# Depthwise taps moved off TensorE, four heads' scores at once, and a 64-row second pass in a four-layer block on one core

## The chip, the cores and the metric

The kernel runs on one core of a Trainium2 chip. It is measured in device microseconds for one execution (all eight images), as the median over several executions. Smaller is better. The core has five engines with a queue each: TensorE (PE in the profile, with its weight loads as PEld), VectorE (DVE), ScalarE (ACT), GpSimd (POOL) and SyncE (SP), which here issues every DMA. An engine takes its instructions strictly in the order in which the program wrote them, and semaphores join the engines.

## The reference, cut to what matters

Eight images of 384 channels and 32x32 pixels go through four layers, each `x + layer(groupnorm(x))`: attention with a depthwise term, a selective scan in four directions, a shifted blur, and a second attention. The change touches the first layer only:

```
qkvo = einsum('oc,bchw->bohw', qkvo_w, x) + qkvo_b           # C = 384
lepe = conv(v_ch, lepe_w, 5x5, 'SAME', groups=C) + lepe_b    # 25 taps for each channel
q, k, v: 12 heads of 32 channels, 1024 pixels
attn = softmax(SCALE * einsum('bnqd,bnkd->bnqk', q, k))
res = einsum('bnqk,bnkd->bnqd', attn, v) + lepe
out = einsum('oc,bchw->bohw', proj_w, res * o) + proj_b
```

Layer 1 is the selective scan: 4 directions x 384 channels x 16 states, a first-order recurrence over 1024 pixels, so 192 scans of 128 channels x 1024 pixels per image.

## The kernel before

**Stages.** All data is float32. The program is a software pipeline over images. While image i goes through its 192 scan steps (layer 1), image i+1 is taken through layer 0 ("early" events) and image i-1 through the layers 2 and 3 ("late" events). Image 0's layer 0 comes first, with nothing beside it; then seven stretches in which a scan and a layer 0 overlap; then the last image's scan with only late work beside it. Each event has a due time in scan steps (`early_events`, `late_events`, `scan_events`); `in_order` sorts them, and every engine writes its share of that one order into its queue. So nothing is dynamic: an event that waits holds up all that stands behind it on its engine.

**A scan step** i is: SP loads two rows of 1024 numbers, broadcast to 128 partitions, into `rows_b` and `rows_c` (`SLOTS` buffers each, at due times i-SLOTS+1.0 and i-SLOTS+2.3); ScalarE makes `decay` (three buffers, L1233, due i-1.25); VectorE makes `drive` = dtu x row into PSUM (L1620, due i+0.40) and runs the scan (L1630, due i+0.90); GpSimd multiplies the state by the other row (L1345), and waits for the next step's drive before it does so; TensorE transposes the product into a running sum (L984).

**Layer 0 of one image** runs three groups of four heads one after the other. Each has two stages.
- The *S stage* (14 steps): scores are made once, only for their row maxima. `S` (L855) makes two heads' 128x512 scores in PSUM banks 0 and 1, `R` (L1560, VectorE) reduces them to maxima, and the next `S` waits for that `R`. There are 32 such pairs in a group. Beside them the depthwise term is summed on TensorE in banks 2 and 3: for each of the 25 taps ScalarE makes a diagonal matrix (`dg`, L1167) and TensorE multiplies a shifted window of the padded v with it (`dw`, L902, two matmuls of 512 columns); `dh` (L1162) copies the sum into `heads`. The padded v itself comes from `tv` (eight transposes, L758) and `pv` (L1182), and `vz` (L1556) zeroes the padding once for each image.
- The *T stage* (16.2 steps): `N`, `M` and `mr` bring the maxima into a row of the moved copy of q; that row, as contraction row 33, subtracts the maximum. `T` (L875) makes transposed scores of two heads in banks 0 and 1, `E` (L1174) exponentiates them into SBUF, `V` (L886) and `Z` (L891) multiply with v and with ones, 32 columns for a head, and `O` (L1567 to L1571) divides and adds to `heads`. There are 32 `T` in a group, 16 `V` and 16 `Z`.

Once in 16 steps new step sizes are made (`x`, `d`: L957, L967, also through bank 0), and three times in an image a finished column sum is turned (`m`: L758, L1601, L1606).

Of the kernel before, what the change touches and what calls it, by code (L numbers as in the profile page):

```python
# [298 lines left out]
def build(nc, t):  # L299
    ctx = ExitStack()  # L300
    with ctx:
# [835 lines left out]
        def _(act):  # L1137
# [10 lines left out]
            def early(img, kind, a=0, j=0, scans=1, first=False):  # L1148
# [11 lines left out]
                if kind == "dh":  # L1160
                    act.wait_ge(dg_ps.h, dg_ps.at(img, TAPS * (a + 1)))
                    act.activation(heads[:, a, :], banks(2), ACT.Copy).then_inc(dh_sb.h, 1)  # L1162
                if kind == "dg":
                    m = a
                    if j >= DIAGS:
                        act.wait_ge(dg_ps.h, dg_ps.at(img, TAPS * m + j - DIAGS + 1))
                    act.activation(diag[m][j % DIAGS], ident[:, :], ACT.Copy, scale=lepe_w[:, m * TAPS + j:m * TAPS + j + 1])\  # L1167
                        .then_inc(dg_sb.h, 1)
# [629 lines left out]
```

## Time and profile before

| | us |
|---|---|
| median of 3 runs | 11385.86 (11383.32 to 11387.95) |
| the profiled execution, whole | 11378.4 |
| its span, first to last instruction | 11376.6 |
| TensorE busy | 8954.9 (79%) |
| VectorE busy | 7592.8 (67%) |
| GpSimd busy | 3956.4 (35%) |
| ScalarE busy | 3900.4 (34%) |
| granted TensorE clock, mean | 0.813 |

One stretch of the loop, from an image's first S stage to the next image's, takes 1344.8 us, and the profile shows the same length, within half a microsecond, for the last five of them.

### The profile page before, as it was taken

What the parts mean: (1) busy time and instruction counts of PE and PEld (TensorE: products, weight loads), DVE (VectorE), ACT (ScalarE), POOL (GpSimd) and SP (SyncE); (2) the same over time, 40 slices, a digit from 0 to 9 for tenths busy, and PEclk for the clock granted to TensorE, in tenths of its full rate; (3) what the DMA queues carried; (4) which work ended last, traced back from release to release, by engine and by line L of the source; (5) the groups of instructions that cost most, each with busy time, mean ns of one, the idle gap of its engine ahead of it and who ended that gap; (6) DMA issues with size and microseconds to landing.
All of it is one profiled execution on the core that took longest, in us unless ns stands there. A gap on an engine that the chain in (4) does not pass through costs nothing.

```text
span 11376.6 us, 106333 instructions
## 1 busy us (share of the span) xinstructions
PE 8954.9 (79%) x36120; PEld 4204.5 (37%) x36120; DVE 7592.8 (67%) x5637; ACT 3900.4 (34%) x4474; POOL 3956.4 (35%) x1678
## 2 busy tenths in 40 slices
PE   6985888588886888768896788858898688877556
PEld 2223333343334433344333433334333443334433
DVE  3127667866677667776668666686677766687892
ACT  1113344333333333432443334333333323343331
POOL 0004333433334333442334333343234423343560
PEclk8665888788886898778886888868898789878657
DMA  1006444744457444664447534474445744466782
GB/s 34 4 19 207 154 144 166 245 172 143 140 179 241 156 141 152 216 200 149 148 148 244 193 129 156 163 244 164 136 148 190 225 155 141 153 225 195 246 267 65
DMA packets 717974, 1876.29 MB, mean 165 GB/s; under 512 B 258897, under 2 KB 274641, under 8 KB 717265
## 3 DMA queue, kind: packets, MB, share of 16 engines
q1 hardware_dynamic: 717392, 1869.00, 49.4%
q8 instruction: 309, 5.06, 0.2%
q14 instruction: 273, 2.23, 0.1%
HBM read 1772.03 MB, written 71.04 MB: 162 GB/s over the span
## 4 chain that ended last, share of the span: by engine, by line
PE 57%; DVE 25%; issue 7%; ACT 5%; DMA 2%; DVEq 2%; SPq 1%; ACTq 1%; POOL 0%; POOLq 0%
DVE R L1630 11%; PE ps L902 9%; PE ps L875 8%; PE ps L748 8%; PE ps L855 7%; PE ps L984 7%; DVE ps L1620 6%; PE ps L886 4%; ACT R L1174 3%; PE ps L1069 3%; DVE nmx L1560 2%; PE ps L1052 2%; PE ps L891 1%; PE ps L957 1%; PE ps L981 1%
## 5 line engine op out<-in xcount | busy, mean ns | idle before, releaser
L1345 POOL TENSOR_TENSOR R<-R 128x1024 f32<-128x1024 f32 x1536 | 3659.8, 2383 | 5546.8 <-DVE ps L1620 5546.8
L1630 DVE TENSOR_TENSOR_SCAN R<-R,ps 128x1024 f32<-128x1024 f32 x1536 | 3508.1, 2284 | 440.1 <-ACT R L1233 334.1
L1233 ACT ACTIVATE R<-R,negA 128x1024 f32<-128x1024 f32 x1536 | 1749.9, 1143 | 2946.0 <-DVE R L1630 2908.6
L984 PE MATMUL ps<-ident,R 128*128 128x128 f32 x12288 | 2068.0, 327 | 588.1 <-POOL R L1345 547.5
L984 PEld LDWEIGHTS ps<-ident,R 128*128 128x128 f32 x12288 | 1746.1, 171 | 1512.1 <-POOL R L1345 753.3
L1620 DVE TENSOR_TENSOR ps<-R 128x1024 f32<-128x1024 f32 x1536 | 1993.1, 1298 | 109.3 <-DVE R L1630 4.7
L1560 DVE TENSOR_REDUCE nmx<-ps 128x2 f32<-128x1024 f32 x768 | 936.4, 1219 | 850.1 <-PE ps L855 843.9
L902 PE MATMUL ps<-R 128*128 128x512 f32 x2400 | 1258.6, 648 | 0.0
L1174 ACT ACTIVATE R<-ps 128x1024 f32<-128x1024 f32 x768 | 785.8, 1023 | 1325.6 <-PE ps L875 1325.6
L875 PE MATMUL ps<-R 33*128 33x512 f32 x3072 | 1048.0, 765 | 173.9 <-ACT R L1174 88.4
L855 PE MATMUL ps<-R 32*128 32x512 f32 x3072 | 939.4, 690 | 198.9 <-DVE nmx L1560 164.6
L748 PE MATMUL ps<-R 128*128 128x512 f32 (+1 forms) x1824 | 873.9, 637 | 202.6 <-DVE R L1498 143.5
L1567 DVE RECIPROCAL R<-ps 128x512 f32<-128x512 f32 x48 | 161.2, 3358 | 797.2 <-PE ps L891 797.2
L902 PEld LDWEIGHTS ps<-R 128*128 128x128 f32 x2400 | 434.4, 202 | 651.1 <-issue 559.3
L748 PEld LDWEIGHTS ps<-R 128*128 128x128 f32 (+1 forms) x1824 | 354.9, 199 | 661.8 <-issue 598.1
L886 PE MATMUL ps<-R 128*32 128x512 f32 x3072 | 508.6, 741 | 51.3 <-DVE R L1569 48.6
L875 PEld LDWEIGHTS ps<-R 33*128 33x128 f32 x3072 | 270.9, 215 | 703.7 <-ACT R L1174 556.0
L855 PEld LDWEIGHTS ps<-R 32*128 32x128 f32 x3072 | 243.5, 193 | 768.6 <-DVE nmx L1560 543.3
L891 PE MATMUL ps<-R,ones 128*32 128x512 f32 x3072 | 466.9, 684 | 0.0
L1337 POOL TENSOR_TENSOR R<-R 128x1024 f32<-128x1024 f32 x96 | 253.2, 2638 | 608.8 <-DVE R L1611 608.8
L1211 ACT ACTIVATE R<-ps,vecs 128x512 f32<-128x512 f32 x192 | 131.3, 684 | 802.1 <-PE ps L967 796.2
L740 PE MATMUL ps<-gn_t,group_avg 128*128 128x1 f32 x672 | 140.9, 338 | 330.4 <-DVE gn_t L1481 277.4
(154 smaller groups left out, 5749.7 us busy)
## 6 DMA issues: line engine op xcount, KB each, us to landing
R<-bc_scratch SPq DMA_DIRECT2D x3072, 512.0 KB, 4.7
R<-in_x SPq DMA_DIRECT2D x72, 512.0 KB, 6.8
out<-R SPq DMA_DIRECT2D x72, 512.0 KB, 5.2
R<-shift_scratch SPq DMA_DIRECT2D x48, 640.0 KB, 7.4
R<-R SPq DMA_DIRECT2D x192, 128.0 KB
R<-out SPq DMA_DIRECT2D x48, 512.0 KB, 8.4
R<-in_w_qkvo SPq DMA_DIRECT2D x32, 576.0 KB, 6.7
rows_scratch<-R SPq DMA_DIRECT2D x24, 512.0 KB, 7.3
```

The source lines that it names most:

```text
L748: mm = pe.matmul(dst[0:parts, hf * HALF:(hf + 1) * HALF], lhs[:, c], rhs(c, hf), start=c == 0, stop=c == NC - 1)
L855: mm = pe.matmul(ps[:, r % 2, :], q4[HD * r:HD * r + HD, g, qc * P:(qc + 1) * P], k4[HD * r:HD * r + HD, g, hf * HALF:(hf + 1) * HALF], st ...
L875: mm = pe.matmul(ps[:, bank + j, :], k2[pair][rows, kb * P:(kb + 1) * P], q2[g][pair][rows, qh * HALF:(qh + 1) * HALF], start=True, stop=True)
L886: pe.matmul(ps[HD * r:HD * r + HD, 2, :], vT[:, kb, P * g + HD * r:P * g + HD * r + HD], pT[(2 * a + r // 2) % 4][:, r % 2, :], start=kb = ...
L902: mm = pe.matmul(ps[:, 2 + hf, :], diag[m][j % DIAGS], win, start=j == 0, stop=j == TAPS - 1)
L984: mm = pe.matmul(ps[:, 4 + b // 4, (b % 4) * P:(b % 4 + 1) * P], state[i % HELD][:, b * P:(b + 1) * P], ident[:, :], start=fresh and i % G ...
L1174: act.activation(pT[a % 4].rearrange("p j q -> p (j q)"), banks(bank), ACT.Exp).then_inc(t_exp.h, 1)
L1233: act.activation(decay[i % len(decay)], dt[:, c, :], ACT.Exp, scale=negA[:, col:col + 1]).then_inc(a_sb.h, 1)
L1345: pool.tensor_tensor(state[i % HELD], state[i % HELD], rows_c[slot], ALU.mult).then_inc(hc_sb.h, 1)
L1560: v.tensor_reduce(nmx4[:, 2 * pair:2 * pair + 2, qc, hf], ps[:, 0:2, :], AX.X, ALU.max, negate=True)\
L1620: v.tensor_tensor(drive, dtu[:, c, :], rows_b[slot], ALU.mult).then_inc(b_sb.h, 1)
L1630: v.tensor_tensor_scan(h, a, b, 0.0, ALU.mult, ALU.add).then_inc(h_sb.h, 1)
```

## The change

Five things are changed in layer 0, and one in the scan.

1. `S` makes the scores of all four heads at once, in banks 0 to 3 (four matmuls of 32 rows each, 16 times a group instead of 32 times two), and `R` reduces 128x2048 at once, 16 times.
2. The taps leave TensorE. For the first 14 (`SUMMED`) ScalarE multiplies the shifted window by the tap (`dp`), the first one straight into `heads`, the others into two buffers `tapped`; GpSimd adds each of the 13 others to `heads` (`dw`, with a drain of GpSimd ahead of it). The last 11 are multiply-adds on VectorE (`dv`), spread over the T stage. `dg`, `dh` and the 25x2 matmuls of each group are gone.
3. As banks 2 and 3 hold scores now, the first `S` of a group waits until `pv` has emptied them.
4. `T` contracts over 64 rows instead of 33. The rows past 33 are zero in `k2`; `vz` zeroes one of the two `k2` buffers for each image, ahead of the padding, and SP's `q2` waits for that.
5. `pv` of a later group waits for the last `dv` of the group before.
6. `SLOTS` goes from 4 to 3: the two buffers `tapped` lie in what were the fourth row buffers.

```diff
-SB = 4 * LB
+SB = 2 * LB
-SLOTS = 4
+SLOTS = 3
-TAPS, DIAGS = 25, 8
+TAPS, SUMMED = 25, 14
...
-        for j in range(TAPS):
-            t = at + 1.0 + (S_STEPS - 1.4) * j / TAPS
-            ev += [(t - 1.0, ("dg", g, j)), (t, ("dw", g, j))]
+        for j in range(SUMMED):
+            t = at + 0.3 + (S_STEPS - 0.6) * j / SUMMED
+            ev += [(t, ("dp", g, j))] + ([(t + 1.0, ("dw", g, j))] if j else [])
...
+        ev += [(at + 0.7 + T_STEPS * j / (TAPS - SUMMED), ("dv", g, SUMMED + j)) for j in range(TAPS - SUMMED)]
...
+        tapped = [reg(at * K1, K1) for at in (15, 19)]
...
                     if a % SB:
                         pe.wait_ge(s_max.h, s_max.at(img, a))
-                    elif g:
+                    else:
+                        pe.wait_ge(lv_sb.h, lv_sb.at(img, g + 1))
+                    if a % SB == 0 and g:
                         pe.wait_ge(t_exp.h, t_exp.at(img, TB * g))
-                    for r in (2 * pair, 2 * pair + 1):
-                        mm = pe.matmul(ps[:, r % 2, :], q4[HD * r:HD * r + HD, g, qc * P:(qc + 1) * P],
+                    for r in range(GH):
+                        mm = pe.matmul(ps[:, r, :], q4[HD * r:HD * r + HD, g, qc * P:(qc + 1) * P],
                                        k4[HD * r:HD * r + HD, g, hf * HALF:(hf + 1) * HALF], start=True, stop=True)
...
-                        rows = slice(64 * j, 64 * j + HD + 1)
+                        rows = slice(64 * j, 64 * j + 64)
...
-                    for hf in range(2):
-                        win = vp[:, j // 5 + 16 * hf:j // 5 + 16 * hf + 16, j % 5:j % 5 + WW]
-                        mm = pe.matmul(ps[:, 2 + hf, :], diag[m][j % DIAGS], win, start=j == 0, stop=j == TAPS - 1)
-                    mm.then_inc(dg_ps.h, 1)
...
+                        if n > 2:
+                            act.wait_ge(dw_sb.h, dw_sb.at(img, n - 2))
+                        act.activation(tapped[n % 2].rearrange("p (h w) -> p h w", w=WW), win, ACT.Copy, scale=tap)\
+                            .then_inc(dp_sb.h, 1)
...
                     if m:
-                        act.wait_ge(dg_ps.h, dg_ps.at(img, TAPS * m))
+                        act.wait_ge(dv_sb.h, dv_sb.at(img, m))
...
+                if kind == "dw":
+                    n = (SUMMED - 1) * m + j
+                    pool.drain()
+                    pool.wait_ge(dp_sb.h, dp_sb.at(img, SUMMED * m + j + 1))
+                    pool.tensor_tensor(heads[:, m, :], heads[:, m, :], tapped[n % 2], ALU.add).then_inc(dw_sb.h, 1)
...
+                    v.wait_ge(qk_sb.h, qk_sb.at(img, 6))
+                    v.memset(k2[0], 0.0)
                     v.memset(vpad, 0.0).then_inc(vz_sb.h, 1)
...
-                    v.tensor_reduce(nmx4[:, 2 * pair:2 * pair + 2, qc, hf], ps[:, 0:2, :], AX.X, ALU.max, negate=True)\
+                    v.tensor_reduce(nmx4[:, :, qc, hf], ps[:, 0:4, :], AX.X, ALU.max, negate=True)\
...
+                if kind == "dv":
+                    m = a
+                    out = heads[:, m, :].rearrange("p (h w) -> p h w", w=WW)
+                    win = vpad.rearrange("p (h w) -> p h w", w=36)[:, j // 5:j // 5 + HH, j % 5:j % 5 + WW]
+                    v.drain()
+                    if j == SUMMED:
+                        v.wait_ge(dw_sb.h, dw_sb.at(img, (SUMMED - 1) * (m + 1)))
+                    ins = v.scalar_tensor_tensor(out, win, lepe_w[:, m * TAPS + j:m * TAPS + j + 1], out, ALU.mult, ALU.add)
```

**Place 1: VectorE in the third S stage.** Before, this is its queue (L1560 is the reduction of two heads, L1620 the drive, L1630 the scan; the names left and right of the arrow are what is written and read, and REGISTER_ALU only works out a wait's value):

```order
L1559 REGISTER_ALU
L1560 TENSOR_REDUCE nmx<-ps 128x2
L1620 TENSOR_TENSOR ps<-R 128x1024
L1559 REGISTER_ALU
L1560 TENSOR_REDUCE nmx<-ps 128x2
L1625 REGISTER_ALU
L1630 SCALAR_TENSOR_TENSOR R<-R,ps 128x1024
L1559 REGISTER_ALU
L1560 TENSOR_REDUCE nmx<-ps 128x2
L1559 REGISTER_ALU
L1560 TENSOR_REDUCE nmx<-ps 128x2
```

Of the changed kernel, the same stage (L1571 is the reduction of four heads, L1641 the drive, L1651 the scan):

```order
L1570 REGISTER_ALU
L1571 TENSOR_REDUCE nmx<-ps 128x4
L1636 REGISTER_ALU
L1641 TENSOR_TENSOR ps<-R 128x1024
L1570 REGISTER_ALU
L1571 TENSOR_REDUCE nmx<-ps 128x4
L1646 REGISTER_ALU
L1651 SCALAR_TENSOR_TENSOR R<-R,ps 128x1024
L1641 TENSOR_TENSOR ps<-R 128x1024
L1570 REGISTER_ALU
L1571 TENSOR_REDUCE nmx<-ps 128x4
```

Where two or three reductions stood around a drive and a scan, one stands now; here and there two reductions have only the drive between them.

**Place 2: GpSimd in the third S stage.** Before, only the state products (L1345):

```order
L1344 REGISTER_ALU
L1345 TENSOR_TENSOR R<-R 128x1024
L1344 REGISTER_ALU
L1345 TENSOR_TENSOR R<-R 128x1024
L1341 REGISTER_ALU
```

Of the changed kernel (L1340 is the state product, L1347 the addition of a tap):

```order
L1339 REGISTER_ALU
L1340 TENSOR_TENSOR R<-R 128x1024
L1346 REGISTER_ALU
L1347 TENSOR_TENSOR R<-R 128x1024
L1339 REGISTER_ALU
L1340 TENSOR_TENSOR R<-R 128x1024
L1346 REGISTER_ALU
L1347 TENSOR_TENSOR R<-R 128x1024
```

An addition has come between nearly every two state products.

**Place 3: VectorE in the third T stage.** Before, drives and scans alone, but for the two `O`:

```order
L1630 SCALAR_TENSOR_TENSOR R<-R,ps 128x1024
L1620 TENSOR_TENSOR ps<-R 128x1024
L1625 REGISTER_ALU
L1630 SCALAR_TENSOR_TENSOR R<-R,ps 128x1024
L1620 TENSOR_TENSOR ps<-R 128x1024
```

Of the changed kernel (L1590 is a tap's multiply-add):

```order
L1651 SCALAR_TENSOR_TENSOR R<-R,ps 128x1024
L1590 SCALAR_TENSOR_TENSOR R<-R,lepe_w 128x1024
L1641 TENSOR_TENSOR ps<-R 128x1024
L1646 REGISTER_ALU
L1651 SCALAR_TENSOR_TENSOR R<-R,ps 128x1024
L1641 TENSOR_TENSOR ps<-R 128x1024
L1590 SCALAR_TENSOR_TENSOR R<-R,lepe_w 128x1024
L1646 REGISTER_ALU
L1651 SCALAR_TENSOR_TENSOR R<-R,ps 128x1024
```

The taps stand in turn ahead of a drive, and between a drive and its scan.

## Rows read from the trace of the kernel before

**Rows 1.** The page: busy time, and the chain that ended last, by engine.

```profile
PE 8954.9 (79%) x36120; PEld 4204.5 (37%) x36120; DVE 7592.8 (67%) x5637; ACT 3900.4 (34%) x4474; POOL 3956.4 (35%) x1678
...
PE 57%; DVE 25%; issue 7%; ACT 5%; DMA 2%; DVEq 2%; SPq 1%; ACTq 1%; POOL 0%; POOLq 0%
```

**Rows 2.** Windows: start:end and length, busy us of PE, PEld, DVE, ACT, POOL, clock, DMA.

```profile
129.50:226.70 97.20, 87.73 (x229) 27.77 (x228) 39.69 (x34) 11.29 (x27) 0.00 (x0) 0.95 0.05 11
231.50:355.20 123.70, 121.46 (x384) 23.11 (x384) 4.74 (x3) 32.77 (x32) 0.00 (x0) 0.51 0.00 0
...
595.80:698.20 102.40, 92.88 (x229) 29.00 (x228) 39.45 (x33) 11.30 (x27) 0.00 (x0) 0.88 0.01 2
703.30:828.40 125.10, 122.79 (x384) 23.24 (x384) 4.74 (x3) 32.77 (x32) 0.00 (x0) 0.50 0.00 0
5398.80:5511.20 112.40, 99.31 (x545) 35.81 (x546) 68.94 (x40) 59.54 (x60) 44.57 (x19) 0.91 0.54 178
5644.60:5759.10 114.50, 105.99 (x540) 35.29 (x540) 66.46 (x38) 60.76 (x63) 44.50 (x19) 0.88 0.53 176
5886.80:6001.10 114.30, 107.24 (x533) 36.72 (x533) 66.43 (x38) 58.75 (x59) 44.59 (x19) 0.84 0.48 166
5258.50:5393.40 134.90, 117.78 (x369) 46.45 (x368) 91.93 (x66) 34.53 (x54) 37.30 (x16) 0.89 0.36 123
5517.30:5639.30 122.00, 108.83 (x357) 44.08 (x356) 89.76 (x66) 33.62 (x52) 35.19 (x15) 0.91 0.34 117
5764.40:5881.50 117.10, 103.09 (x337) 41.02 (x336) 89.31 (x64) 32.84 (x51) 35.19 (x15) 0.92 0.35 124
```

**Rows 3.** Groups by line: engine, operation, count, busy us, mean ns, idle before.

```profile
L902 PE MATMUL ps<-R 128*128 128x512 f32 x2400 | 1258.6, 648 | 0.0
...
L1560 DVE TENSOR_REDUCE nmx<-ps 128x2 f32<-128x1024 f32 x768 | 936.4, 1219 | 850.1 <-PE ps L855 843.9 <-issue 1.0
...
L1182 ACT ACTIVATE R<-ps,vecs 128x1024 f32<-128x1024 f32 x24 | 27.1, 1128 | 151.8 <-PE ps L758 97.5 <-DVE R L1556 54.4
```

**Rows 4.** Steps of the scan alone: two drives in order of time.

```profile
6095.65 1.23 DVE L1620 TENSOR_TENSOR ps<-R 128x1024 f32<-128x1024 f32 x1
...
6099.38 1.23 DVE L1620 TENSOR_TENSOR ps<-R 128x1024 f32<-128x1024 f32 x1
```

**Rows 5.** An S stage in order of time: start us, length, what, idle before and releaser.

```profile
5262.57 2.08 PE L855 MATMUL ps<-R 32*128 32x512 f32 x4 [2.94 <-DVE nmx L1560]
...
5274.90 1.28 DVE L1601 SCALAR_TENSOR_TENSOR R<-R,derived,ps 128x1024 f32<-128x1024 f32 x1 [4.43 <-PE ps L758]
...
5334.79 2.36 POOL L1345 TENSOR_TENSOR R<-R 128x1024 f32<-128x1024 f32 x1
...
5336.26 1.98 DVE L1620 TENSOR_TENSOR ps<-R 128x1024 f32<-128x1024 f32 x1
...
5338.15 1.21 DVE L1560 TENSOR_REDUCE nmx<-ps 128x2 f32<-128x1024 f32 x1
...
5339.29 2.27 DVE L1630 TENSOR_TENSOR_SCAN R<-R,ps 128x1024 f32<-128x1024 f32 x1
```

**Rows 6.** Single lines: shortest, median and longest in ns.

```profile
L1620 DVE TENSOR_TENSOR ps<-R x1536: 1216/1234/3881, 937.4 to 11095.7; 128x1024 f32<-128x1024 f32 x192
...
L1586 DVE SCALAR_TENSOR_TENSOR R<-R,derived x24: 1283/1285/3108, 846.2 to 10076.4; 128x1024 f32<-128x1024 f32 x24
```

**Rows 7.** Image 0, first T stage, in order of time.

```profile
273.60 2.08 PE L875 MATMUL ps<-R 33*128 33x512 f32 x4
...
277.48 2.08 PE L875 MATMUL ps<-R 33*128 33x512 f32 x4
```

**Rows 8.** A loop T stage at full clock, in order of time.

```profile
5704.68 1.13 PE L875 MATMUL ps<-R 33*128 33x512 f32 x4
...
5707.99 1.06 PE L886 MATMUL ps<-R 128*32 128x512 f32 x8
```

**Rows 9.** The loads of the drive's rows (SP, L599): issue to landing.

```profile
DMA to landing us min/median/max: 3.2/4.7/13.1
```

More of the change, by code:

```diff
@@ L380, in build @@
         vpad = side(14336, 36 * 36)
-        diag = [[side(9216 + K1 * g + P * i, P) for i in range(DIAGS)] for g in range(GROUPS0)]
         rinv = [side(HALF * i, HALF) for i in range(2 * GROUPS0)]
@@ L472, in build @@
         pv_ps = sem("products_done", GROUPS0 * TB // 2)
-        dg_sb = sem("tap_diagonal_ready", TAPS * GROUPS0)
-        dg_ps = sem("tap_summed", TAPS * GROUPS0)
-        dh_sb = sem("depthwise_term_ready", GROUPS0)
+        dp_sb = sem("tap_product_ready", SUMMED * GROUPS0)
+        dw_sb = sem("tap_summed", (SUMMED - 1) * GROUPS0)
+        dv_sb = sem("depthwise_term_ready", GROUPS0)
         o_sb = sem("heads_divided", 2 * GROUPS0)
@@ L667, in early @@
                     if g == 0:
-                        sp.wait_ge(s_ps.h, s_ps.at(img, 1))
+                        sp.wait_ge(vz_sb.h, vz_sb.at(img, 1))
                         for pair in range(2):
@@ L845, in early @@
                 if kind == "S":
-                    g, qc, hf, pair = a // SB, a % SB // 4, a % 4 // 2, a % 2
+                    g, qc, hf = a // SB, a % SB // 2, a % 2
                     if a == 0:
@@ L879, in early @@
                     g, qh, kb = a // (2 * LB), a // LB % 2, a % LB
-                    if kb == 0 and qh == 0:
-                        pe.wait_ge(dh_sb.h, dh_sb.at(img, g + 1))
                     if kb == 0 and qh == 1:
@@ L1159, in early @@
                             .then_inc(qk_sb.h, 1)
[L1160 to L1168, printed above, removed]
+                if kind == "dp":
+                    m, n = a, (SUMMED - 1) * a + j
+                    win = vpad.rearrange("p (h w) -> p h w", w=36)[:, j // 5:j // 5 + HH, j % 5:j % 5 + WW]
+                    tap = lepe_w[:, m * TAPS + j:m * TAPS + j + 1]
+                    if j == 0:
+                        act.wait_ge(lv_sb.h, lv_sb.at(img, m + 1))
+                        act.activation(heads[:, m, :].rearrange("p (h w) -> p h w", w=WW), win, ACT.Copy, scale=tap)\
+                            .then_inc(dp_sb.h, 1)
+                    else:
+                        if n > 2:
+                            act.wait_ge(dw_sb.h, dw_sb.at(img, n - 2))
+                        act.activation(tapped[n % 2].rearrange("p (h w) -> p h w", w=WW), win, ACT.Copy, scale=tap)\
+                            .then_inc(dp_sb.h, 1)
                 if kind == "E":
@@ L1352, in late @@
                     norm(img, u)
-            norm(0, "attn0")
-            norm(0, "scan")
+            for ev in in_order(early_events()):
+                if ev[0] == "ne":
+                    norm(0, ev[1])
+                elif ev[0] == "dw":
+                    early(0, *ev)
             for ev in in_order(first_scan_events()):
@@ L1363, in _ @@
                     norm(1, ev[1])
+                elif ev[0] == "dw":
+                    early(1, *ev)
             with pool.Fori(1, B - 1) as img:
@@ L1369, in _ @@
                         norm(img + 1, ev[1])
+                    elif ev[0] == "dw":
+                        early(img + 1, *ev)
                     elif is_late(ev):
@@ L1565, in early @@
                     v.wait_ge(pv_ps.h, pv_ps.at(img, LB * (a + 1)))
-                    v.wait_ge(dh_sb.h, dh_sb.at(img, g + 1))
+                    v.wait_ge(dw_sb.h, dw_sb.at(img, (SUMMED - 1) * (g + 1)))
                     v.reciprocal(rinv[a], ps[:, 3, :])
@@ L1711, in _ @@
             v.memset(negm[:, :], 0.0)
+            v.memset(k2[1], 0.0)
             v.memset(ones[:, :], 1.0)
```

14 lines of the change are left out of this document (6 added, 8 removed).

## The prediction

> **What bounds the kernel now.** I read the page first, then windows cut at the stages, then single lines in order of time. TensorE is busy for 79% of the span and holds 57% of the chain that ended last, VectorE 25% [rows 1]. That is a mean over stages, so I read each stage by itself. In the three S stages of a loop image TensorE is busy 118, 109 and 103 us of 135, 122 and 117, VectorE about 90 to 92 in each [rows 2]. There the two alternate: a reduction, then the next scores, and between scores the tap matmuls, 50 in a group (2400 rows are 24 groups x 50 x 2, as a float32 matmul shows as two rows, 0.65 us each) [rows 3]. VectorE idles before L1560 for 850 us in total, nearly all of it until L855 is done [rows 3]. So the S stages are bound by TensorE. In the T stages TensorE is busy 99 to 107 of 112 to 114 us and VectorE 66 to 69 [rows 2]: TensorE again, with some 45 us of slack on VectorE. Outside both (some 640 of an image's 1344.8 us) nothing of the change but the row buffers counts.
>
> **The granted clock.** The S and T stages of the loop run at 0.84 to 0.92 on average, so 16 to 32% of a stage is at 1.2 GHz. Image 0's T stages are the odd ones: TensorE is busy for 121.5 of 123.7 us and yet the clock is 0.51, while the S stage ahead of it has 0.95 [rows 2]. `T` takes 2.08 us there and one `T` with its `V` or `Z` 3.87 us [rows 7], where at full clock they take 1.13 and 1.06 [rows 8]. What stands in those stages is `T` on 33 rows of a tile and `V`, `Z` on 32 columns, and no full-size matmul.
>
> **The change, part by part.** I sum against the profiled execution, 11378.4 us, which lies 7.5 under the median.
>
> *S stage in the loop (21 of them).* Off TensorE go 50 tap matmuls and half of the score passes. What is left for it in a step is one transposed product and 1.14 score passes, so VectorE sets the pace. A step of scan alone takes 3.73 us (two drives) [rows 4]; a reduction of 128x1024 takes 1.14 until the next instruction starts [rows 5], so one of 128x2048 about 2.25 (not over twice 1.14, not under 1.9). 14 x 3.73 + 16 x 2.25 = 88 us. To that come:
> - the third stage: 1.4 for a dt sum and the minimum. As TensorE is little busy, I expect 1.2 GHz, where scores take 2.08 [rows 5]. Where only the drive stands between two reductions (twice in a stage, place 1) VectorE waits about 1 us; two step-size matmuls put 1.5 each in that path. GpSimd's additions: below, 6. Sum 88 + 1.4 + 2 + 3 + 6 = 100.5.
> - the second: a column merge besides, 2.5 busy and 7 waiting (4.43 before L1601 now [rows 5], more at the lower clock): 110.
> - the first: two row projections more. It is 12.9 us longer than the second now [rows 2], a part of it being the zeroing; I keep 8: 118.
>
> Together 328.5 against 374.0 [rows 2], so 45 less for each image, 7 images: **-315**. Bounds: VectorE's own busy time and no waits give -70 for an image, every wait doubled -20.
>
> *GpSimd against VectorE.* A drive that starts while GpSimd runs is held: 1.98 us instead of 1.23, its end 1.1 after GpSimd's; the longest is 3.88; L1586, like `dv` a multiply-add with two SBUF inputs, goes from 1.28 to 3.11. The scan and the reductions beside it keep their length [rows 5, 6]. In a step of the new S stage GpSimd starts the state product when the drive ends (2.36 us), then the addition (2.36, the same form), so it is free 4.8 us after the drive. VectorE comes to the next drive after scan and reduction, 2.28 + 2.25 = 4.5 us. So I charge 0.25 for a step and 2.4 once, where two additions stand between two state products: 6 us. The drain of GpSimd shows in no row; I take it as free, and at the most as 1 us. ScalarE's 14 products of about 1.13 us (L1182, the nearest) [rows 3] replace 25 short ones and find it busy 33 to 35 us of a stage [rows 2]: hidden.
>
> *Start of a group.* The first scores now wait for `pv`, 1.13 us, and for the zeroing of `k2` in front of it. 5 us in the first group, 1.5 in the others: 8 x 8 = **+64**. Bounds 2 and 12 for an image.
>
> *T stage.* 11 `dv` a group. Six stand ahead of a drive (GpSimd's product just ends, 1.4 us each), five between a drive and its scan, where GpSimd starts first: 1.28 + 2.3 = 3.6 each. 26 us onto 66 leaves VectorE at 92 of 114. TensorE still sets the pace; as decays and `E` share ScalarE's queue a part will leak: +3 a stage, x 21 = +63 (bounds 0 and 10). On 64 rows `T` does the same passes in the same time. If the rows also bring the clock up, what is at 1.2 GHz now (2 x 0.09 x 112, 2 x 0.12 x 114, 2 x 0.16 x 114 = 84 us in an image, of which 39 are the cold starts after `N`) loses half of 45: -22 an image. With VectorE as full as that I take half, -11 x 7 = -78. Sum **-15**.
>
> *Image 0.* S stage: 16 x (2.25 + 2.08 + 0.1) = 71 against a mean of 100 [rows 2, 5]: **-87**. T stage at full clock: 32 x 2.25 = 72, plus the wait for `O`, 76 against 124: **-144**.
>
> *Three row buffers.* A row lands 4.7 us after its issue in the median and 13.1 at the longest [rows 9]. Three steps of scan alone are 11.2 us, less one drive 10, so the median is covered and the tail, in the late-layer loads, isn't: 4 us an image, **+32** (bounds 0 and 80).
>
> **Sum.** -315 + 64 - 15 - 87 - 144 + 32 = -465: 11378.4 - 465 = 10,913, and 10,920 on the median's scale.
>
> **On the clock,** the Trainium skill ("TensorE: Matmul & The Clock Gate", Part 1) says that the gate follows how busy TensorE has been. By that rule image 0's T stages, 98% busy, should have had the full clock; the trace shows 0.51. So the rule as it stands doesn't decide this case. If busy time were all, 64 rows would change nothing, which is the second rival below.
>
> **The rivals.**
> - *The clock doesn't follow the rows* (0.27). For it: nothing in the trace has 64-row tiles, and `V` and `Z`, half of the time, stay as they are. Against it: image 0's S stages, with full-size tap matmuls, run at 0.88 to 0.95 and its T stages at 0.51 [rows 2]. It takes away 144 and 78: 11,140.
> - *VectorE bounds the T stage* (0.10). 92 of 114 us is a mean; if the `dv` that stand between drive and scan pass half of their 18 us on, a T stage gains nothing from the clock and grows by 10: +210 instead of -15, 11,145.
> - *Four row tiles don't run side by side* (0.04). For it: the trace has only pairs. Against it: `V` puts four column tiles through in 1.06 us [rows 8]. If four took twice as long, a score pass would be 4.2 us at 1.2 GHz, against 3.5 that a drive and a scan cover: 1 us more for each of 16 passes in 21 stages, 2.1 in image 0's three, +436: 11,350, about as before.
> - *GpSimd becomes the bound of the S stage, and the kernel is slower* (0.05). The chain is drive, state product, addition, drive: 1.23 + 2.36 + 2.36 = 5.95 us with nothing between [rows 5]. Fourteen are 83 us, with merges and projections 95. An S stage is 124.7 now, and the other terms (-150) give 7 us more to each, so the kernel is slower from (131.8 - 95) / 13 = 2.8 us of drain and hand-over for an addition on; at 3.5 us it takes 11,560. Against it: where one engine hands over to another in the S stage, scores to a reduction, it costs about 0.1 us. For it: no row has a drain of GpSimd.
> - The rest (0.02) is no visible change.
>
> **How the numbers follow.** My case has 0.52. Its own range comes from the bounds of the S stage (-175, +175), taken half, and of the row buffers: 10,740 to 11,060. Two rivals lie at 11,140, so the range that leaves out 2 in 10 is 10,680 (every S wait hidden, and the T stages' clock gain whole) to 11,180. A measurement of this kernel tells about 0.2% (23 us) from no change. Faster: 0.52 + 0.27 + 0.10 + 0.03 for the tiles = 0.92; same 0.02; slower 0.05 for GpSimd and 0.01 for the tiles = 0.06.
>
> **What would show it.** Right: VectorE's idle time before the reductions falls from 850 us to under 200; S stages of 118, 110 and 100 us with a granted clock of 0.5 to 0.6; reductions of about 2.3 us; GpSimd busy about 740 us more (312 additions x 2.36) and drives held by a few tenths; image 0's T stages of 76 us at a clock near 0.95. Wrong: T stages of image 0 still at 0.51; drives of 3 us in the S stages; scans that wait for row loads; T stages over 120 us.

## The result, and the profile after

| | before | after |
|---|---|---|
| median, us | 11384.59 (4 runs, 11382.62 to 11387.95) | 10545.74 (4 runs, 10530.69 to 10569.52) |
| profiled execution, whole | 11378.4 | 10569.5 |
| ratio of the medians | | 0.9265, 95% interval 0.9246 to 0.9283 |

The changed kernel is 839 us (7.4%) faster; the forecast was 10,920 with a range of 10,680 to 11,180. The sign was right, and the gain was not quite twice the forecast. The profiled execution is the longest of the four, 24 us over the median, so a term read from its trace is good to some 20 us.

The page of the changed kernel: busy time, and the chain that ended last by engine (to compare with [rows 1]).

```profile
PE 7395.8 (70%) x33720; PEld 3735.7 (35%) x33720; DVE 8085.9 (77%) x5526; ACT 4057.7 (38%) x4186; POOL 4790.4 (45%) x1990
...
PE 41%; DVE 31%; issue 14%; ACT 7%; DMA 4%; DVEq 2%; SPq 1%; ACTq 1%; POOL 0%; POOLq 0%
```

TensorE lost 1559 us of work, VectorE took 493 more, GpSimd 834 more. VectorE is now the busiest engine. The windows of image 0's first S and T stage, then of one loop image's three S stages and its three T stages (columns as in [rows 2]):

```profile
132.80:205.10 72.30, 33.44 (x128) 8.27 (x128) 36.91 (x17) 15.99 (x14) 30.49 (x13) 0.50 0.07 15
210.00:282.50 72.50, 68.92 (x384) 15.89 (x384) 15.08 (x13) 32.63 (x32) 0.00 (x0) 0.95 0.00 1
4799.80:4905.60 105.80, 62.20 (x268) 27.95 (x268) 90.35 (x48) 39.96 (x41) 67.66 (x28) 0.71 0.44 146
5028.80:5128.80 100.00, 59.64 (x256) 30.20 (x256) 90.20 (x49) 39.27 (x39) 71.04 (x28) 0.64 0.43 145
5245.90:5342.10 96.20, 55.33 (x236) 26.75 (x236) 87.85 (x48) 38.60 (x38) 72.05 (x28) 0.61 0.48 157
4911.00:5021.80 110.80, 97.71 (x545) 34.46 (x546) 90.50 (x51) 59.51 (x60) 43.45 (x19) 0.93 0.48 171
5134.10:5238.60 104.50, 95.66 (x540) 32.61 (x540) 89.32 (x49) 60.72 (x63) 42.25 (x18) 0.98 0.52 178
5347.70:5455.00 107.30, 96.55 (x533) 34.25 (x533) 87.92 (x49) 58.49 (x59) 43.80 (x19) 0.94 0.53 177
```

In the S stages TensorE fell from 103 to 118 us busy to 55 to 62, and VectorE fills 88 to 90 of 96 to 106: the bound changed hands. In the T stages TensorE still sets the pace, at a granted clock of 0.93 to 0.98 instead of 0.84 to 0.91, and VectorE rose from 66 to 69 us to 88 to 91. Image 0's T stage went from 123.7 us at 0.51 to 72.5 at 0.95.

Two groups of the page (columns as in [rows 3]):

```profile
L1571 DVE TENSOR_REDUCE nmx<-ps 128x4 f32<-128x2048 f32 x384 | 877.0, 2284 | 298.8 <-PE ps L858 295.2
...
L1347 POOL TENSOR_TENSOR R<-R 128x1024 f32<-128x1024 f32 x312 | 822.9, 2637 | 401.5 <-ACT R L1162 339.8
```

VectorE's idle time before the reductions fell from 850 us to 299, not under 200. GpSimd's 312 additions took 823 us.

**The span by stages.** An S stage runs here from a group's first scores to the end of its minimum (L1595), a T stage from its first `T` to its last `Z`; image 0 ends with the first scan; the loop is seven images. All are from profiled executions, in us. The last image's scan, 1193 to 1197 in all, makes up the span.

| kernel | median | span | image 0 | loop S stage, mean of 21 | loop T stage, mean of 21 | rest of the loop |
|---|---|---|---|---|---|---|
| before | 11384.6 | 11376.6 | 941.4 | 124.7 | 113.2 | 4246 |
| b_rows64 | 11097.0 | 11104.8 | 792.9 | 125.2 | 106.9 | 4246 |
| b_slots3 | 11400.3 | 11399.1 | 954.0 | 124.9 | 114.4 | 4227 |
| after | 10545.7 | 10567.7 | 709.7 | 100.2 | 107.0 | 4310 |
| a_rows33 | 10833.2 | 10825.4 | 867.3 | 100.0 | 112.6 | 4300 |
| a_pairs | 11310.7 | 11300.8 | 820.9 | 131.3 | 106.5 | 4292 |
| a_smalladds | 10493.9 | 10500.4 | 708.6 | 98.0 | 106.3 | 4306 |
| a_dvahead | 10545.8 | 10537.3 | 710.1 | 100.2 | 106.2 | 4299 |
| a_dvbetween | 10663.6 | 10665.7 | 708.3 | 100.0 | 108.5 | 4384 |
| a_steps12 | 10539.4 | 10537.1 | 709.7 | 96.1 | 107.4 | 4359 |
| a_dv12 | 10475.0 | 10469.8 | 710.4 | 96.0 | 107.6 | 4290 |
| a_dv10 | 10504.0 | 10501.4 | 708.1 | 89.8 | 112.3 | 4357 |
| a_tv0 | 10524.2 | 10518.5 | 704.9 | 100.8 | 106.8 | 4262 |
| a_dvtv | 10481.7 | 10491.4 | 703.9 | 97.9 | 108.1 | 4268 |

From before to after, over unrounded stages: S stages of the loop -516, T stages -128, image 0 -232, rest of the loop +63, last image +3, together -809.

### The profile page after: what moved, and what is told of

The parts are those of the page before. It is cut to its first block, busy times and chain, and to the rows that moved or that the text cites. A ratio compares the mean times of both kernels' runs of the same rounds, so it can differ in the third digit from the quotient of the medians.

```text
span 10567.7 us, 101292 instructions
## 1 busy us (share of the span) xinstructions
PE 7395.8 (70%) x33720; PEld 3735.7 (35%) x33720; DVE 8085.9 (77%) x5526; ACT 4057.7 (38%) x4186; POOL 4790.4 (45%) x1990
## 3 DMA queue, kind: packets, MB, share of 16 engines
q14 instruction: 289, 2.36, 0.1%
## 4 chain that ended last, share of the span: by engine, by line
PE 41%; DVE 31%; issue 14%; ACT 7%; DMA 4%; DVEq 2%; SPq 1%; ACTq 1%; POOL 0%; POOLq 0%
DVE R L1651 14%; PE ps L749 8%; DVE ps L1641 7%; PE ps L878 7%; PE ps L975 5%; ACT R L1169 4%; DVE nmx L1571 3%; PE ps L1060 3%; PE ps L887 3%; PE ps L858 3%; PE ps L948 2%; PE ps L1043 2%; PE ps L958 1%; PE ps L843 1%; PE ps L1032 1%
## 5 line engine op out<-in xcount | busy, mean ns | idle before, releaser
L1340 POOL TENSOR_TENSOR R<-R 128x1024 f32<-128x1024 f32 x1536 | 3676.4, 2394 | 4304.6 <-DVE ps L1641 4194.3
L1651 DVE TENSOR_TENSOR_SCAN R<-R,ps 128x1024 f32<-128x1024 f32 x1536 | 3507.8, 2284 | 178.9 <-ACT R L1228 65.8
L975 PE MATMUL ps<-ident,R 128*128 128x128 f32 x12288 | 2153.8, 336 | 584.0 <-POOL R L1340 542.2
L1641 DVE TENSOR_TENSOR ps<-R 128x1024 f32<-128x1024 f32 x1536 | 2025.4, 1319 | 163.0 <-DMA R<-bc_scratch 56.7
L858 PE MATMUL ps<-R 32*128 32x512 f32 x3072 | 687.3, 979 | 754.6 <-DVE nmx L1571 662.3
L1571 DVE TENSOR_REDUCE nmx<-ps 128x4 f32<-128x2048 f32 x384 | 877.0, 2284 | 298.8 <-PE ps L858 295.2
L878 PE MATMUL ps<-R 64*128 64x512 f32 x3072 | 917.8, 676 | 204.9 <-ACT R L1169 107.2
L1347 POOL TENSOR_TENSOR R<-R 128x1024 f32<-128x1024 f32 x312 | 822.9, 2637 | 401.5 <-ACT R L1162 339.8
L1590 DVE SCALAR_TENSOR_TENSOR R<-R,lepe_w 128x1024 f32<-128x1024 f32 x264 | 512.7, 1942 | 28.1 <-issue 6.2
L858 PEld LDWEIGHTS ps<-R 32*128 32x128 f32 x3072 | 172.7, 266 | 994.6 <-DVE nmx L1571 844.8
L1162 ACT ACTIVATE R<-R,lepe_w 128x1024 f32<-128x1024 f32 x312 | 360.7, 1159 | 352.9 <-POOL R L1347 352.8
L878 PEld LDWEIGHTS ps<-R 64*128 64x128 f32 x3072 | 244.2, 194 | 641.9 <-ACT R L1169 418.0
L887 PE MATMUL ps<-R 128*32 128x512 f32 x3072 | 432.2, 636 | 55.2 <-DVE R L1580 51.4
L1332 POOL TENSOR_TENSOR R<-R 128x1024 f32<-128x1024 f32 x96 | 253.0, 2636 | 441.6 <-DVE R L1632 441.6
L759 PE MATMUL ps<-ident,R 128*128 128x128 f32 x1280 | 215.4, 325 | 231.1 <-DVE R L1670 71.5
```

Of the source, the lines that this page charges most:

```text
L858: mm = pe.matmul(ps[:, r, :], q4[HD * r:HD * r + HD, g, qc * P:(qc + 1) * P], k4[HD * r:HD * r + HD, g, hf * HALF:(hf + 1) * HALF], start= ...
L878: mm = pe.matmul(ps[:, bank + j, :], k2[pair][rows, kb * P:(kb + 1) * P], q2[g][pair][rows, qh * HALF:(qh + 1) * HALF], start=True, stop=True)
L887: pe.matmul(ps[HD * r:HD * r + HD, 2, :], vT[:, kb, P * g + HD * r:P * g + HD * r + HD], pT[(2 * a + r // 2) % 4][:, r % 2, :], start=kb = ...
L975: mm = pe.matmul(ps[:, 4 + b // 4, (b % 4) * P:(b % 4 + 1) * P], state[i % HELD][:, b * P:(b + 1) * P], ident[:, :], start=fresh and i % G ...
L1340: pool.tensor_tensor(state[i % HELD], state[i % HELD], rows_c[slot], ALU.mult).then_inc(hc_sb.h, 1)
L1347: pool.tensor_tensor(heads[:, m, :], heads[:, m, :], tapped[n % 2], ALU.add).then_inc(dw_sb.h, 1)
```

## The experiments

Names that begin with b_ are the kernel before with a part of the change, those with a_ the changed kernel with an edit. Ratios are to the kernel before on the same chip.

**b_rows64: the 64-row second pass alone** (with the zeroing of `k2` and SP's wait for it).

```diff
-                        rows = slice(64 * j, 64 * j + HD + 1)
+                        rows = slice(64 * j, 64 * j + 64)
```

> The kernel before with the 64-row second pass alone (and the zeroing that it needs). Theory: the gain in the T stages comes from the clock, and the rows alone bring it: image 0's T stages fall from 124 us at 0.51 to about 73 near 1.0 (-153), the loop's T stages from a mean of 114 to 105 or below, since no taps wait on VectorE there (-9 x 21 = -190): about 11,040. Rival: the T stages became shorter since TensorE, ScalarE and PSUM no longer carry taps ahead of them; then 64 rows alone change nothing: 11,384.

Measured 11097.0 (11093.3 to 11106.6), ratio 0.9747 [0.973, 0.9763]. Its windows of image 0's first T stage and of the loop's third:

```profile
236.30:307.90 71.60, 68.22 (x384) 15.87 (x384) 4.74 (x3) 32.74 (x32) 0.00 (x0) 0.96 0.00 1
...
5689.60:5794.00 104.40, 93.67 (x533) 32.20 (x533) 66.41 (x38) 58.48 (x59) 44.53 (x19) 0.97 0.54 182
```

The same 384 matmul rows as before, in 71.6 us at 0.96 instead of 123.7 at 0.51. The first rival (the clock doesn't follow the rows) fell; the theory stands, if some 60 us short of its number. Image 0 gave 148 us, the 21 T stages 132, and the S stages took 9 back. The zeroing of `k2` takes 0.91 us once for each image, in the first S stage. It doesn't account for the 9 us: the first S stages became 3.3 us shorter, the second and third 1.6 and 2.9 longer. Why is open.

**a_rows33: the changed kernel on 33 rows**, the same edit backwards.

> The changed kernel with the second pass back on 33 rows. Theory of the clock: image 0's T stages return to 124 us at 0.51 (+155) and the loop's to 113 or more (+6 x 21 = +126): 10,545 + 281 = 10,826. Rival, that the rows do nothing: 10,545.

Measured 10833.2 (10827.2 to 10836.5), ratio 0.9517 [0.9501, 0.9533]. Image 0's first T stage and the loop's third:

```profile
210.70:335.50 124.80, 122.56 (x384) 23.32 (x384) 15.10 (x12) 32.76 (x32) 0.00 (x0) 0.50 0.00 1
...
5549.90:5664.40 114.50, 107.72 (x533) 37.35 (x533) 87.93 (x49) 58.71 (x59) 43.94 (x19) 0.83 0.49 166
```

So the rows are worth 288 us in either kernel: this part adds to the others and doesn't depend on them.

**b_slots3: three row buffers alone** (`SLOTS = 3`).

> The kernel before with three row buffers instead of four, nothing else. Theory now: the drives and products have enough lead with three, within 5 us of before (11,384). Rival, as predicted: 4 us for each image, 11,416.

Measured 11400.3 (11389.2 to 11411.9), ratio 1.0012 [1.0003, 1.0022], so +14 (0.3 to 2.2 in a thousand). It lies between the two. Drives that never waited for a row before now do so 23 times, for 54 us in all; most of that was slack. Nor are the 14 us shown to come from rows: in the traces, 22 us apart, 12.6 us of the difference lie in image 0, which ends with the first scan, so before any drive.

**a_pairs: scores of two heads at a time, all else as in the changed kernel.**

```diff
-SB = 2 * LB
+SB = 4 * LB
...
-                    for r in range(GH):
-                        mm = pe.matmul(ps[:, r, :], q4[HD * r:HD * r + HD, g, qc * P:(qc + 1) * P],
+                    for r in (2 * pair, 2 * pair + 1):
+                        mm = pe.matmul(ps[:, r % 2, :], q4[HD * r:HD * r + HD, g, qc * P:(qc + 1) * P],
```

> The changed kernel with the scores of two heads at a time again (32 passes and 32 reductions a group), taps as changed. Theory: the width of the reduction matters as much as the taps, as each pass exposes a round trip to TensorE at the lower clock: image 0's S stage is 32 x (1.23 + 2.1 + 0.1) = 110 instead of 72 (+113), the loop's S stages 118 instead of 100 (+380): 11,040. Rival: with the taps gone TensorE has room, reductions of either width fill VectorE alike, and it costs under 3 us a stage: below 10,610 plus what image 0 loses.

Measured 11310.7 (11293.8 to 11334.7), ratio 0.994 [0.9923, 0.9957]: 765 us above the changed kernel, and 214 above b_rows64. The 214 us are what moving the taps does by itself (with the later start and three row buffers): it makes the kernel slower. The third S stage, a pair's scores and VectorE's reductions in it:

```profile
5678.10:5803.50 125.40, 94.44 (x236) 37.48 (x236) 88.79 (x63) 38.34 (x38) 66.28 (x28) 0.50 0.36 123
```

```profile
5692.35 2.08 PE L858 MATMUL ps<-R 32*128 32x512 f32 x4
```

```profile
L1571 DVE TENSOR_REDUCE nmx<-ps 128x2 f32<-128x1024 f32 x32 | 39.2, 1225 | 36.6 <-PE ps L858 36.6
```

With the tap matmuls, full-size, this stage ran at 0.92 before and at 0.90 in b_rows64; without them the granted clock is 0.50, where a pair's scores take 2.08 us, and the reductions of the 32 rounds wait 36.6 us for scores, against 27.8 before. Sixteen rounds of four heads wait 7.1. That the lower clock makes the difference between 27.8 and 36.6 is read from these rows; no run changes the clock alone. I expected 11,040. That had the lower clock in it and image 0 right (110 us a stage for 109), but the 118 us for the loop's S stages were not worked out, and they took 131. Those 131 us, above the 125 of the kernel before, are the clearest evidence that moving the taps pays only together with four heads at a time.

**a_smalladds: GpSimd's additions on 8 of 1024 columns.**

```diff
-pool.tensor_tensor(heads[:, m, :], heads[:, m, :], tapped[n % 2], ALU.add)
+pool.tensor_tensor(heads[:, m, 0:8], heads[:, m, 0:8], tapped[n % 2][:, 0:8], ALU.add)
```

> The changed kernel, but each of GpSimd's tap additions adds 8 of 1024 columns, so the depthwise term is left incomplete; waits, order and ScalarE's products stay. Theory: the additions cost VectorE only the holding of drives, 2.5 us an S stage in the loop (drives took 20.8 us where 15 x 1.22 are 18.3), 21 stages: 10,545 - 53 = 10,490; image 0 unchanged. Rival, as predicted, GpSimd's share is 6 us a stage or more: 10,420 or below.

Measured 10493.9 (10479.3 to 10502.9), ratio 0.9213 [0.9198, 0.9229], -52 as expected. The drives in the third S stage, of the changed kernel and then of this one:

```profile
L1641 DVE TENSOR_TENSOR ps<-R 128x1024 f32<-128x1024 f32 x15 | 20.8, 1390 | 0.7
```

```profile
L1641 DVE TENSOR_TENSOR ps<-R 128x1024 f32<-128x1024 f32 x14 | 17.2, 1228 | 0.7
```

The additions cost VectorE 0.16 us a drive, 2.2 us an S stage.

**a_dvahead and a_dvbetween: where the multiply-adds stand.** All eleven ahead of the drive of their step, or all between a drive and its scan.

```diff
-ev += [(at + 0.7 + T_STEPS * j / (TAPS - SUMMED), ("dv", g, SUMMED + j)) for j in range(TAPS - SUMMED)]
+ev += [(int(at + 0.7 + T_STEPS * j / (TAPS - SUMMED)) + 0.95, ("dv", g, SUMMED + j)) for j in range(TAPS - SUMMED)]
```

(a_dvbetween has 0.6 in the place of 0.95.)

> The changed kernel with every multiply-add of VectorE due right ahead of a drive (due time k + 0.95), none between a drive and its scan. Theory: TensorE still bounds the T stages and the multiply-adds cost them only some 1 us; busy time of the 11 falls from 22.7 us to under 17 a stage, and the time by 0 to 25 us: 10,530. Rival: VectorE bounds the T stages; then what is no longer held comes off: 5 us a stage, 10,440.

> The changed kernel with all eleven dv of a group put between a drive and its scan, where GpSimd's product runs beside them and each is held to about 3.4 us: 37 us in a T stage instead of 23 to 26, so VectorE is busy about 101 of 107 us. Rival 2 of the prediction (VectorE bounds the T stage, half of the added 13 us is passed on): +6.5 us in each of 21 stages, 10,680. The theory that held so far (VectorE's slack takes it, as moving them ahead of the drive changed nothing): 10,550 to 10,570. I expect the rival's side, since only 6 us of slack are left: 10,640.

Measured 10545.8 (10539.1 to 10558.8), ratio 0.9267 [0.9251, 0.9282], no change; and 10663.6 (10659.3 to 10667.5), ratio 0.9365 [0.935, 0.9381], +118. All `dv`, shortest, median and longest in ns, of the changed kernel and then of a_dvbetween:

```profile
L1590 DVE SCALAR_TENSOR_TENSOR R<-R,lepe_w x264: 1283/1285/3444, 206.1 to 9216.7; 128x1024 f32<-128x1024 f32 x132
```

```profile
L1590 DVE SCALAR_TENSOR_TENSOR R<-R,lepe_w x264: 1283/3421/3447, 204.7 to 9316.8; 128x1024 f32<-128x1024 f32 x132
...
5384.30:5493.00 108.70, 96.46 (x533) 33.98 (x533) 98.23 (x48) 58.49 (x59) 41.83 (x18) 0.94 0.49 172
```

In the last six loop images (the first has no late layers beside it) VectorE is busy 8 to 10 us less in a T stage of a_dvahead, which is worth nothing, and 5 to 10 us more in one of a_dvbetween, which costs 118 in all. Of 104 to 112 us it is busy 88 to 91 in the changed kernel and 95 to 98 in a_dvbetween; its slack ends somewhere between. In the trace, 98 us longer, 31 lie in the T stages (1.5 each) and 74 in the rest: VectorE leaves a T stage one drive and scan behind and comes late to the next group. The T stage of a_dvbetween that ends at 5044.9, and what follows it:

```profile
5049.52 3.35 DVE L1578 RECIPROCAL R<-ps 128x512 f32<-128x512 f32 x1
...
5056.88 2.09 PE L858 MATMUL ps<-R 32*128 32x512 f32 x8 [1.22 <-ACT R L1177]
```

The scores come 11.9 us after the last `Z`, 7.0 in the changed kernel (rows below). The rival mechanism (VectorE bounds the T stage) is real, but the change stops short of it.

The Trainium skill ("SBUF — State Buffer", "SBUF: two separate sides") says that a VectorE operation with two SBUF inputs and a GpSimd operation that reads SBUF exclude each other for a whole instruction. The trace agrees: a multiply-add takes 1.28 us alone and 3.43 when a state product of 2.36 started 0.01 us ahead of it (the first two rows below), so it ends 1.08 us after the product.

**a_steps12, a_dv12, a_dv10: scan steps moved from the S stages to the T stages.** 12 and 18.2 steps instead of 14 and 16.2; the same with `dv` as in a_dvahead; and 10 and 20.2 with it.

```diff
-S_STEPS, N_STEPS, T_STEPS = 14, 1.6, 16.2
+S_STEPS, N_STEPS, T_STEPS = 12, 1.6, 18.2
```

> The changed kernel with S stages of 12 scan steps instead of 14 and T stages of 18.2 instead of 16.2. Theory: the S stages are bound by VectorE now, so two steps less are 2 x 3.7 us less; the T stages are bound by TensorE with VectorE at 88 of 107 us, and two steps more cost them only two transposed products and hand-overs, 3 us: -4.5 x 21 = -95, 10,450. Rival: both stages are bound by VectorE (or S still by the round trip to TensorE), and the steps just move: 10,545.

> Both edits, 12 steps in the S stage and the multiply-adds ahead of drives. Theory: with 18 steps in the T stage VectorE is closer to full there, so that the held multiply-adds matter more than alone: 10,420, 30 us below the one with 12 steps alone. Rival: no more than the one with 12 steps.

> The changed kernel with S stages of 10 steps of scan and T stages of 20.2, and dv ahead of the drives (one step further than the run with 12 and 18.2). Theory (VectorE bounds the S stage, the T stage has slack on it): an S stage 4 us shorter, a T stage 1 longer, so -60 against 12 and 18.2: 10,415. Rival (with fewer scans beside them the 16 rounds of scores and reduction set the pace of the S stage, and T stages grow by 2 to 4): 10,480 to 10,500.

Measured 10539.4 (10527.0 to 10550.7), ratio 0.9257 [0.9242, 0.9272]; 10475.0 (10462.3 to 10482.7), ratio 0.92 [0.9185, 0.9216]; 10504.0 (10503.2 to 10505.2), ratio 0.9227 [0.9211, 0.9242].

My expectation for a_steps12 (10,450) fell. An S stage and a T stage together came out near it, 3.7 us shorter where I had 4.5, though not for its reasons: the S stage lost 4.1 instead of 7.4 and the T stage gained 0.4 instead of 3. But the rest grew by 50. The end of the first T stage of a_steps12 in order of time:

```profile
4992.80 2.36 POOL L1340 TENSOR_TENSOR R<-R 128x1024 f32<-128x1024 f32 x1 [1.39 <-DVE ps L1641]
...
4992.81 3.43 DVE L1590 SCALAR_TENSOR_TENSOR R<-R,lepe_w 128x1024 f32<-128x1024 f32 x1
...
4997.97 1.07 PE L892 MATMUL ps<-R,ones 128*32 128x512 f32 x8
...
4999.88 2.29 DVE L1651 TENSOR_TENSOR_SCAN R<-R,ps 128x1024 f32<-128x1024 f32 x1
...
5003.41 3.35 DVE L1578 RECIPROCAL R<-ps 128x512 f32<-128x512 f32 x1
...
5010.77 2.09 PE L858 MATMUL ps<-R 32*128 32x512 f32 x8 [1.22 <-ACT R L1177]
```

and of the changed kernel:

```profile
5020.75 1.06 PE L892 MATMUL ps<-R,ones 128*32 128x512 f32 x8
...
5021.88 3.36 DVE L1578 RECIPROCAL R<-ps 128x512 f32<-128x512 f32 x1 [1.51 <-PE ps L892]
...
5026.06 1.55 PE L759 MATMUL ps<-ident,R 128*128 128x128 f32 x8 [3.22 <-DVE R L1580]
...
5027.65 1.13 ACT L1177 ACTIVATE R<-ps,vecs 128x1024 f32<-128x1024 f32 x1 [6.90 <-PE ps L759]
5028.83 2.09 PE L858 MATMUL ps<-R 32*128 32x512 f32 x8 [1.22 <-ACT R L1177]
```

After the last `Z` the start of a group is one chain: `O` (reciprocal and product), the turn of v, `pv`, the scores. In the changed kernel VectorE waits for that `Z` (1.51 us idle) and the scores come 7.0 us after its end. In a_steps12 a late `dv`, held to 3.43 us, leaves VectorE behind, and the reciprocal starts 4.4 us after the end of `Z`; the scores come after 11.7. The third group of this image starts 2.7 us later too. Over the seven loop images the second groups start 3.9 us later in the mean and the third ones 2.2 (the first image shows almost nothing of it), 43 of the 50 us. With `dv` ahead of the drives the rest is back at 4290, and a_dv12 is faster than the changed kernel and than a_steps12 (its interval meets neither of theirs). With 10 steps the S stages shrink by another 6.2 us each, but T stages grow by 4.7 and the rest by 66 in all: 12 is the better split of the three.

**a_tv0 and a_dvtv: the turn of v out of that chain.** v of the next group is turned into banks 0 and 1, right behind the last `V`, while VectorE still divides; a_dvtv is that with the edits of a_dv12.

```diff
-        ev += [(at - 0.05, ("tv", g)), (at - 0.04, ("pv", g))]
+        ev += [(at - (1.15 if g else 0.05), ("tv", g)), (at - (1.12 if g else 0.04), ("pv", g))]
...
-                        pe.wait_ge(o_sb.h, o_sb.at(img, 2 * m))
-                    turn_blocks(2, lambda b: vT[:, b, m * P:(m + 1) * P]).then_inc(lv_ps.h, 1)
+                        pe.wait_ge(t_exp.h, t_exp.at(img, TB * m))
+                    turn_blocks(0 if m else 2, lambda b: vT[:, b, m * P:(m + 1) * P]).then_inc(lv_ps.h, 1)
```

> The changed kernel with the eight transposes of the next group's v (tv) and their evacuation (pv) moved from banks 2 and 3 to banks 0 and 1 and placed right behind the last V, so that they run while VectorE divides (O); the first scores then wait for O alone. Theory (the start of a group is a chain O, tv, pv, scores on the path): the first scores come 2.4 to 2.8 us earlier after the last Z, 2 starts in each of 8 images, so -42 us against the changed kernel: 10,504. Rival (the start is hidden by the scan beside it, or the step-size matmuls that use bank 0 are put off by as much): 10,546.

> Both: S stages of 12 steps, T stages of 18.2, dv ahead of the drives, and the next group's v turned in banks 0 and 1. If the gains add, 10,475 - 42 = 10,433; if the start of a group hides behind the scan, 10,475.

Measured 10524.2 (10520.3 to 10543.9), ratio 0.925 [0.9234, 0.9265], and 10481.7 (10472.7 to 10493.2), ratio 0.9204 [0.9189, 0.922]. The same place in a_tv0 (L761 is the turn, L896 `Z`, L1582 the reciprocal, L862 the scores):

```profile
4987.39 1.09 PE L761 MATMUL ps<-ident,R 128*128 128x128 f32 x8
...
4989.28 1.06 PE L896 MATMUL ps<-R,ones 128*32 128x512 f32 x8
...
4990.41 3.36 DVE L1582 RECIPROCAL R<-ps 128x512 f32<-128x512 f32 x1 [2.38 <-PE ps L896]
...
4994.68 2.09 PE L862 MATMUL ps<-R 32*128 32x512 f32 x8 [3.31 <-DVE R L1584]
```

The scores come 4.3 us after the last `Z`, as meant, and the rest of the loop is 48 us shorter in the trace. Of the median only 22 are left, which the intervals don't tell from none, and on top of a_dv12 nothing is left: there the rest gives 23 us and the S stages take 40 back. A likely reason, not tested, is that VectorE does the same work either way and only meets it at another place. The rival in the expectation (what else uses bank 0 is put off by as much) isn't ruled out either.

## Why the sign was right and the size wrong

**The S stages of the loop: the step that failed.** The term was -315 and measured -516. The mechanism was as put (TensorE gives the pace to VectorE; four row tiles run side by side: 2.09 us for four heads, as for two in [rows 5], so that rival fell); the sum of 100.5, 110 and 118 us was too large, where image 4 shows 96.2, 100.0 and 105.8:
- *The base and its waits*, two errors that nearly cancelled. 14 x 3.73 + 16 x 2.25 took a step of scan alone as a step's own work. But 3.73 holds a drive, a scan and 0.2 of hand-overs, as each of the two needs what the other left. A reduction depends on neither, and the drive behind it starts before it has ended, as these rows show (columns as in [rows 5]):

```profile
5256.04 2.29 DVE L1571 TENSOR_REDUCE nmx<-ps 128x4 f32<-128x2048 f32 x1 [2.18 <-PE ps L858]
...
5258.25 1.22 DVE L1641 TENSOR_TENSOR ps<-R 128x1024 f32<-128x1024 f32 x1
...
5259.57 2.29 DVE L1651 TENSOR_TENSOR_SCAN R<-R,ps 128x1024 f32<-128x1024 f32 x1
...
5262.11 2.36 POOL L1347 TENSOR_TENSOR R<-R 128x1024 f32<-128x1024 f32 x1 [0.22 <-DVE R L1651]
```

  The third stage has 87.9 us of VectorE busy, 2.5 of them drives that are held (20.8 us for 15, against 15 x 1.22), so 85.4 of its own work against the 89.4 charged. Its waits are 8.4 us (7.1 before reductions) against the 5 charged. Net -0.6.
- *GpSimd's additions.* Charged 6, measured 2.5 in the trace and 2.2 by a_smalladds. Net -3.5.
- *The merge.* Charged 9.5, of which 7 waiting:

```profile
5034.33 1.27 DVE L1622 SCALAR_TENSOR_TENSOR R<-R,derived,ps 128x1024 f32<-128x1024 f32 x1
...
5037.66 1.22 DVE L1627 COPY R<-ps 128x1024 f32<-128x1024 f32 x1 [2.06 <-PE ps L759]
```

  The first turn is done while VectorE reduces and drives, and only the second is waited for, 2.06 us. The second stage is 3.8 longer than the third, not 9.5.
- *The projections.* Charged 8, measured 5.8.

With the third stage 4.3 short (0.6 + 3.5, and rounding), the merge 5.7 and the projections 2.2, that is 4.3 x 3 + 5.7 x 2 + 2.2 = 26.5 us an image, 185 in the loop, nearly all of the 201 that the term was short. So what failed first of all is two prices: that of GpSimd's additions, worked out from the order of the queues alone, and that of the merge's wait, read at 4.43 in the kernel before and raised to 7. My lower bound of -70 an image was broken too (-74), though 34 us of waits were left. It was called VectorE's own busy time, and stands for 304 us in the three stages; measured, VectorE is busy 268. The sum's own terms without the waits (89.4 x 3, 6 x 3 for GpSimd, 2.5 x 2 for the merges, 8 for the projections) already come to 299: the bound still held what was charged too much there.

**The T stages: two terms mis-sized, both towards slower.** -15 was forecast and -128 measured. The working gave 22 us an image for the clock; I took half, with no row for it. b_rows64 shows 19 and a_rows33 17. For the eleven `dv` I charged 3 us a stage; between b_rows64 (106.9) and the changed kernel (107.0) there is none. I had VectorE's load right (92 forecast, 88 to 91 measured), but at this load nothing leaked, and a_dvbetween shows a load at which it does.

**What held.** Image 0 was forecast at -87, -144 and 8 for the starts, -223, and came to -232 (-84, -155 and 7). The start of a group was forecast at 8 us an image and came to 7.8: an image's first scores come 5.0 us later (counted from the first scan beside it), those of the two later groups 2.8 us later in all (counted from the last `Z`). The clock followed the rows. Image 0's T stage was 72.5 us where I had 76. The granted clock in the loop's S stages was 0.61 to 0.71, where I had 0.5 to 0.6.

**The row buffers.** +32 forecast, +14 alone. Inside the changed kernel, where there is no room for a fourth, it wasn't tried; its rest of the loop grew by 9 us an image, of which the starts take 7.8, so little is left for them.

**GpSimd and a slower kernel.** The rival needed 2.8 us of hand-over for an addition. With its drain an addition starts 0.22 us after the state product (the last of the four rows above; 288 of the 312 together have 59.1 us of such idle time), and GpSimd is busy 72 of 96 us in the third S stage: far from it. Its work grew by 834 us where I had 740, as an addition took 2.64 us in the mean instead of 2.36.

**The range.** Four terms of the own case (GpSimd's additions, the wait for the merge, the clock, the leak) were each set towards slower for caution, so their errors added instead of cancelling, and the median of 10,546 lies 134 us below the lower end of 10,680. That end stood for every S wait hidden and the whole gain of the clock; the waits were not all hidden, and the time was still shorter, since the charges called busy time were too large as well.

## What to carry to other kernels

- When work leaves the busiest engine, build the new stage from the next engine's busy time in the same stage and list the waits singly, each from a row. A step taken from another part of the program carries hand-overs that the new stage may fill; here that error was covered by another, and the prices set above their rows for caution (additions, merge, clock, leak) made up most of what the forecast missed.
- Two parts of a change can be worth +214 us (the taps moved) and -765 (the four heads at a time on top): free the resource (here PSUM banks and TensorE's queue) only together with what uses it, and look at what the freed engine's clock does to the short operations that stay.
- Where stages are joined by a chain over four engines, read the few us around the joint: moving VectorE's work by a fraction of a step was worth nothing in one schedule and 64 us in another.

## What the runs showed of the hardware

- The granted clock depended on the rows that a matmul pass uses, not on busy time alone. TensorE was 98% busy in both 33-row kernels' image 0 T stages at 0.50 to 0.51 and 95% busy in the 64-row ones at 0.95 to 0.96, with the same number of passes of the same length at equal clock (1.13 us for four). The rows past 33 hold zeros in `k2`, the stationary operand; nothing zeroes them in the moving one, so whether it is the count of rows or what streams through them no run tells. The Trainium skill ("TensorE: Matmul & The Clock Gate", Part 1) lets the clock follow how busy the engine has been; by busy share alone the two would have had the same clock, and the trace differs, 124 us against 72.
- Four heads' scores on four row tiles took 2.09 us at 1.2 GHz, as long as two heads' on two.
- A reduction from PSUM of 128x2048 took 2.28 us against 1.22 for 128x1024, and neither the reductions nor the scans were ever held by GpSimd (longest 2.29 us of 384, and of 1536); a multiply-add with two SBUF inputs was held from 1.28 to 3.44.
